# A mixture-of-experts stage between two halves of an attention: fc2's operands exchanged, its result turned on VectorE and stored in 128-byte pieces

## The chip, the cores and the metric

The kernel runs on one core of one Trainium2 chip. The metric is the device time of one execution in microseconds. The kernel before takes 930.86 us, the median of 3 runs (929.11 to 931.17).

## The reference

The input is x, 8 sequences of 1024 tokens with 128 features. It is normalised per token (xn), and the result is the sum of x, of an attention and of a mixture of experts, both of xn:

```
xn  = layernorm(x)
att = gamma * attention(xn) + xn        # 8 heads, q and k of 2 features per head, v of 16,
                                        # scores through leaky relu (0.2), softmax over 1024 keys
# experts: 16 of them, each token goes to its best 2, 1024 slots per expert
xr  = rmsnorm(xn) * norm_weight
probs = softmax(xr @ router.T + router_bias);  gate, expert = top_k(probs, 2)
dispatch[expert, slot] = xr             # 4 experts are trivial (zero, copy, two constant vectors)
h   = gelu(dispatch[4:] @ fc1.T + fc1_bias)          # 12 experts: 1024x128 by 128x512
o   = h @ fc2.T + fc2_bias                           # 1024x512 by 512x128
ffn = sum of the token's two rows of o, weighted by gate / sum of gates
out = x + att + ffn
```

All of it is float32.

## The kernel before

It has five instruction streams written out by hand, one for each engine: the sync engine (`sp`) issues nearly all DMAs in order, GpSimd (`pool`) does the indirect DMAs and the sums into y, ScalarE (`act`) the exponentials and gelus, TensorE (`pe`) the matmuls, and VectorE (`dve`) the rest. Nothing schedules them: on each engine instructions run in the order in which they are written, and the engines wait for each other by semaphores, most of which count instructions or, for a DMA, 16 each.

The program has four stages. A prologue normalises, projects and routes. Then comes the attention of the first three sequences (BH = 3), in which GpSimd scatters the tokens' rows to `disp` in DRAM, 1024 rows of 128 floats per expert. The third stage is the 12 experts. The fourth is the attention of the other five sequences, in which GpSimd gathers the experts' rows from `eout` in DRAM and adds them.

The expert stage is what the change touches. For expert e with u = e % 2:

- The sync engine stores expert e - 2's result and then loads expert e into the buffers of parity u (`store_expert`, `load_expert`, L352 to L367): fc1's weights and fc2's weights, 256 KB each, fc1's bias, fc2's bias spread over all 128 partitions (64 KB), and the expert's rows in four DMAs, each for 32 of the features in pieces of 32 floats (128 bytes). The semaphore `ed0` or `ed1` counts all eight.
- VectorE (`turn_rows`, L1126 to L1133) waits for all of these, multiplies fc1's weights by the norm's weight (L1130) and turns the rows in 32x32 blocks (L1133), so that `xt` holds features in partitions and slots in columns.
- TensorE (`expert`, L880 to L902) multiplies fc1: 8 matmuls with a 128x128 block of weights standing and 512 slots passing (L890); ScalarE takes each through gelu into `hs`, hidden features in partitions and slots in columns (L745). Then fc2: 32 matmuls in which a block of 128 slots of `hs` stands and 128 columns of fc2's weights pass (L901), four to each block of slots, so that the result has slots in partitions.
- VectorE (`expert_rows`, L1138 to L1145) waits for fc2 and for the previous store, and adds the bias from PSUM into `yo` (L1142). This releases the next store.

On VectorE the order in the loop (L1149 to L1152) is: scale and turn expert e + 1, then add expert e's bias. On TensorE the next fc1 follows fc2. In the trace fp32 matmuls stand as two records each.

At the stage's start expert 0 is loaded while the attention still runs. Expert 1 is loaded after the DMAs of `spread` (L328 to L335), 16 small ones that move a pass of attention results between partitions, and after the last value matmul (`pv`). At the end, TensorE computes three score tiles of the next attention between the halves of the last fc2, and VectorE rectifies them (L1112) ahead of the last bias add. `hs`, `yo` and the second row buffer lie in the same memory as the attention's exponentials (`pr`).

Of the kernel before, what the change touches and what calls it, by code (L numbers as in the profile page):

```python
# [8 lines left out]
ALU = mybir.AluOpType  # L9
# [3 lines left out]
P = 128  # L13
B, M, C = 8, 1024, 128
# [10 lines left out]
HALF = 512  # L25
# [9 lines left out]
E, E_MLP, FFN = 16, 12, 512  # L35
FC = FFN // P
CAP = T * 2 // E
SLOTS = E_MLP * CAP
ST = CAP // P
# [22 lines left out]
BLOCK = 32  # L62
NR = P // BLOCK
# [35 lines left out]
    return c  # L99


def build(nc, x, consts, w_qk, b_qk, w_vr, b_v, r_b, n_w, n_w_row, w1t, b1, w2t, b2, cvec, gamma, out):
# [4 lines left out]
    with ExitStack() as ctx:  # L107
        def sb(name, shape, dt=F32):
            return ctx.enter_context(nc.sbuf_tensor(name, shape, dt))

        def sem(name):
# [15 lines left out]
        nwr = sb("nwr", [P, C])  # L127
        gam = sb("gam", [P, 1])
        cv = sb("cv", [P, 2, C])
        b1s = sb("b1s", [P, 2, FC])  # L130
        onesb = sb("onesb", [P, P], BF16)

        bst = sb("bst", [P, NT, 6])
# [47 lines left out]
        gate, rank, at, keep, tmp = (small[:, k:k + 2, :] for k in (4, 6, 8, 10, 12))  # L181


        hs, yo = ef[:, 0:4, :], ef[:, 7, :]
        xt = sb("xt", [P, CAP])
        dd = [xs[:].rearrange("p u t c -> p (u t c)"), ef[:, 5, :]]
        b2s = pflat[:, 0:2 * C].rearrange("p (u c) -> p u c", c=C)
        g1 = xs[:].rearrange("p u (t k) c -> p u t k c", k=2)


# [15 lines left out]
                 "ed0 ed1 w1_rdy xt_rdy fc1 gel fc2 yo_rdy yo_out gath0 gath1 comb final").split()  # L206
        S = {n: sem(n) for n in names}

        block = ctx.enter_context(nc.Block())
# [24 lines left out]
            return slice(2 * HP * (b % 2), 2 * HP * (b % 2) + 2 * HP)  # L234

        ONE = 1
        FROM_ONE = ("gel", "yo_rdy", "yo_out")
        CO0 = 2

        def unit_of(i):  # L240
# [19 lines left out]
        def _(sp):  # L260
# [88 lines left out]
                    spread(p - 1)  # L349
            sp.wait_ge(S["scat"], 16 * GS)  # L350

            def load_expert(e, u):  # L352
                for dst, src in ((w1[:, (2 * u) * FFN:(2 * u + 1) * FFN], w1t[bass.ds(e, 1), :, :].rearrange("a p f -> p (a f)")),
                                 (w1[:, (2 * u + 1) * FFN:(2 * u + 2) * FFN], w2t[bass.ds(e, 1), :, :].rearrange("a p f -> p (a f)")),
                                 (b1s[:, u, :], b1[bass.ds(e, 1), :, :].rearrange("a p f -> p (a f)")),
                                 (b2s[:, u, :], b2[bass.ds(e, 1), :].partition_broadcast(P))):
                    sp.dma_start(dst, src).then_inc(S[f"ed{u}"], 16)
                for q in range(NR):

                    cols = slice(BLOCK * q, BLOCK * q + BLOCK)  # L360
                    sp.dma_start(dd[u][cols, :].rearrange("r (m c) -> r m c", c=BLOCK),
                                 disp[bass.ds(e * CAP, CAP), cols].rearrange("(m r) c -> r m c", r=BLOCK)
                                 ).then_inc(S[f"ed{u}"], 16)

            def store_expert(e):
                sp.wait_ge(S["yo_rdy"], ONE + e + 1)
                sp.dma_start(eout[bass.ds(e * CAP, CAP), :].rearrange("(j p) c -> p j c", p=P),  # L367
                             yo.rearrange("p (j c) -> p j c", c=C)).then_inc(S["yo_out"], 16)

            load_expert(0, 0)  # L370
            spread(BH * NPB - 2)

            sp.wait_ge(S["pv"], BH * NPB * TB)
            load_expert(1, 1)
            with sp.Fori(0, E_MLP // 2 - 1) as k:
                for u in range(2):
                    store_expert(2 * k + u)

                    load_expert(2 * k + u + 2, u)
            for u in range(2):  # L380
                store_expert(E_MLP - 2 + u)

# [13 lines left out]
        def _(pool):  # L396
# [243 lines left out]
            pool.wait_ge(S["yo_out"], ONE + 16 * E_MLP)  # L640
            attention(BH, B, gather)


# [1 line left out]
        def _(act):  # L645
# [81 lines left out]
            def attention(b0, b1):  # L727
                first, end = b0 * NUB, b1 * NUB
                for i in range(first, end):
                    if i == (BUFS - 1) * PAIRS + 1:  # L730
                        act.wait_ge(S["route"], 1)
                    if i == BH * NUB:
                        act.wait_ge(S["fc2"], E_MLP)
                    if i == BH * NUB + (BUFS - 1) * PAIRS:
                        act.wait_ge(S["yo_out"], ONE + 16 * E_MLP)
                    exponentials(i)

            attention(0, BH)
# [24 lines left out]
        def _(pe):  # L763
# [71 lines left out]
            def values(c, half):  # L835

                p, kc = divmod(c, TB)
                hg = p // NQ % NHG
                cols = slice(half * HALF // 2, (half + 1) * HALF // 2)
                pe.wait_ge(S["exps"], PAIRS * (c + 1))  # L840
                if kc == 0 and half == 0:
                    if p == 0:
                        pe.wait_ge(S["at_rdy"], 1)
                    if p == BH * NPB:
                        pe.wait_ge(S["yo_rdy"], ONE + E_MLP)
# [35 lines left out]
            def expert(e, u, first=False, last=False):  # L881
                pe.wait_ge(S["w1_rdy"], e + 1)
                pe.wait_ge(S["xt_rdy"], e + 1)
                for n in range(2 * FC):
                    half, f = n // FC, n % FC

                    pe.wait_ge(S["gel"], ONE + 2 * FC * e + max(n - 3, 0))
                    if n == 2 and first:
                        turn(BH * NPB - 1)
                    pe.matmul(ps[:, 2 + n % 4, :], w1[:, 2 * u * FFN + f * P:2 * u * FFN + (f + 1) * P],  # L890
                              xt[:, half * HALF:(half + 1) * HALF], start=True, stop=True).then_inc(S["fc1"], 1)
                pe.wait_ge(S["turned"], NPB * BH)
                pe.wait_ge(S["yo_rdy"], ONE + e)
                for half in range(2):
                    pe.wait_ge(S["gel"], ONE + 2 * FC * e + FC * (half + 1))
                    if half == 1 and last:
                        ahead(BH, RING)
                    for j in range(half * ST // 2, (half + 1) * ST // 2):
                        o = ps[:, 6 + j // 4, (j % 4) * P:(j % 4 + 1) * P]
                        for f in range(FC):  # L900
                            mm = pe.matmul(o, hs[:, f, j * P:(j + 1) * P],  # L901
                                           w1[:, (2 * u + 1) * FFN + f * P:(2 * u + 1) * FFN + (f + 1) * P],  # L902
                                           start=(f == 0), stop=(f == FC - 1))
                mm.then_inc(S["fc2"], 1)

            ahead(0, AHEAD)
            attention(0, BH)
# [13 lines left out]
        def _(dve):  # L921
# [203 lines left out]

            def turn_rows(e, u):  # L1126

                dve.wait_ge(S[f"ed{u}"], 64 * (e - u) + 128)
# [6 lines left out]
            attention(0, BH)  # L1135


            def expert_rows(e, u):  # L1138

                dve.wait_ge(S["fc2"], e + 1)  # L1140
                dve.wait_ge(S["yo_out"], ONE + 16 * e)
                dve.tensor_tensor(yo.rearrange("p (j c) -> p j c", c=C),  # L1142
                                  ps[:, 6:8, :].rearrange("p a (j c) -> p (a j) c", c=C),
                                  b2s[:, u, :].unsqueeze(1).broadcast_to([P, ST, C]), ALU.add
                                  ).then_inc(S["yo_rdy"], 1)  # L1145

            dve.wait_ge(S["sum_rdy"], 1)
            dve.reciprocal(gsum[:], gsum[:]).then_inc(S["inv_rdy"], 1)
# [12 lines left out]
_INS = ("x", "consts", "w_qk", "b_qk", "w_vr", "b_v", "r_b", "n_w", "n_w_row", "w1t", "b1", "w2t", "b2", "cvec",  # L1161
        "gamma")


def layouts(i):
# [7 lines left out]
    for n, width in (("W", C), ("b", 1)):  # L1173
# [15 lines left out]
        "b1": a["ffn_fc1_bias"].reshape(E_MLP, FC, P).transpose(0, 2, 1),  # L1189
        "w2t": a["ffn_fc2_weight"].transpose(0, 2, 1).reshape(E_MLP, FC, P, C).transpose(0, 2, 1, 3).reshape(E_MLP, P, FC * C),  # L1190
        "b2": a["ffn_fc2_bias"],
        "cvec": a["ffn_constant_vectors"].reshape(1, 2, C),
        "gamma": a["attn_gamma"].reshape(1, 1),
    }
# [18 lines left out]
```

## Time and profile before

| | us |
|---|---|
| median of 3 runs | 930.86 |
| the profiled execution | 931.08 |
| its span, first to last instruction | 929.3 |
| TensorE busy | 851.2 (92%) |
| VectorE busy | 763.9 (82%) |
| ScalarE busy | 676.9 (73%) |
| GpSimd busy | 602.1 (65%) |

The expert stage lies between about 362 and 533 us of the span. A share of busy time over the whole span mixes stages: VectorE is busy almost throughout the attention, and in the expert stage only about a fifth of the time. So the stage is read by itself: by the chain of waits (what each engine was released by), by the engines' instructions in order of time with the idle time ahead of them, and by busy time in short stretches. In these, PEclk is TensorE's granted clock (1.00 is 2.4 GHz), and the DMA share is that of the core's 16 DMA engines.

### The profile page before, as it was taken

The numbers are of one execution on the slowest core, as the hardware profiler recorded it, in microseconds if no ns is written. First come the engines' busy times: TensorE is split into PE (matmuls) and PEld (weight loads), VectorE is DVE, ScalarE is ACT, GpSimd is POOL, SyncE is SP. The second block draws the span as 40 slices with busy tenths as digits, with TensorE's granted clock in tenths as the row PEclk, the third lists the DMA queues.
The fourth block names the chain that finished last, engine by engine and source line by source line (L and its number), as shares of the span: only waits on it lengthen the run. The fifth ranks groups of instructions, "written<-read, shape, count | busy, mean of one in ns | idle before, by whom it ended". The sixth has DMA issues, their size and how long they took to land.

```text
span 929.3 us, 19960 instructions
## 1 busy us (share of the span) xinstructions
PE 851.2 (92%) x7403; PEld 338.5 (36%) x7404; DVE 763.9 (82%) x883; ACT 676.9 (73%) x787; POOL 602.1 (65%) x610
## 2 busy tenths in 40 slices
PE   0687269999999999999999999999999999999997
PEld 0454112222222224776776722222222222222222
DVE  5798899999999996322321399999999999999996
ACT  0578888888888888344344388888888888888886
POOL 3355247777777662999999426567566675766772
PEclk9999669999999999999999999999999999999999
DMA  8733101111111014355364111012112011200202
GB/s 220 301 68 77 31 28 33 49 40 52 50 25 37 21 30 92 88 137 126 86 141 125 40 48 40 21 28 59 29 30 60 25 35 27 77 23 17 68 16 54
DMA packets 130167, 59.34 MB, mean 64 GB/s; under 512 B 83498, under 2 KB 120194, under 8 KB 130080
## 3 DMA queue, kind: packets, MB, share of 16 engines
q1 hardware_dynamic: 120464, 48.06, 20.3%
q0 software_dynamic: 8192, 9.37, 3.7%
q8 instruction: 54, 0.88, 0.4%
q10 hardware_dynamic: 1424, 0.76, 0.4%
q14 instruction: 33, 0.27, 0.1%
HBM read 31.58 MB, written 30.02 MB: 66 GB/s over the span
## 4 chain that ended last, share of the span: by engine, by line
PE 59%; DVE 25%; issue 8%; ACT 3%; POOL 2%; DMA 1%; SPq 1%; POOLq 0%; DVEq 0%; ACTq 0%
DVE ps L1112 20%; PE ps L850 18%; PE ps L830 11%; PE ps L820 11%; PE ps L901 9%; PE ps L890 9%; DVE ot L1088 2%; PE ps L780 1%; DMA y<-in_x 1%; ACT pr L675 1%; DVE bst L947 1%; ACT pr L724 1%; SPq L262 1%; POOL ot L410 1%; ACT va L684 1%
## 5 line engine op out<-in xcount | busy, mean ns | idle before, releaser
L1112 DVE TENSOR_SCALAR ps<-ps 128x1024 f32<-128x1024 f32 x512 | 600.3, 1224 | 15.1 <-PE ps L820 12.1
L724 ACT ACTIVATE pr<-ps 128x1024 f32<-128x1024 f32 x512 | 524.0, 1024 | 104.6 <-PE ps L830 70.7
L850 PE MATMUL ps<-pr,vp 128*32 128x256 f32 x4096 | 327.7, 392 | 0.3
L830 PE MATMUL ps<-q,kz 64*128 64x512 bf16 x1024 | 200.6, 389 | 10.1 <-DVE ps L1112 4.3
L820 PE MATMUL ps<-q,kz 62*128 62x512 bf16 x1024 | 200.8, 390 | 2.9 <-DMA q<-parts_dram 1.4
L511 POOL DMA_INDIRECT xs<-eout,idxs x128 | 129.1, 1008 | 107.5 <-ACT pr L724 82.3
L496 POOL DMA_INDIRECT disp<-xn,idx x128 | 125.8, 983 | 50.4 <-issue 28.2
L745 ACT ACTIVATE pr<-ps,b1s 128x512 f32<-128x512 f32 x96 | 66.0, 687 | 96.4 <-PE ps L890 96.4
L830 PEld LDWEIGHTS ps<-q,kz 64*128 64x128 bf16 x1024 | 48.9, 92 | 226.1 <-DVE ps L1112 187.7
L850 PEld LDWEIGHTS ps<-pr,vp 128*32 128x32 f32 x4096 | 81.1, 108 | 120.5 <-issue 118.1
L1130 DVE TENSOR_SCALAR w<-w,nw 128x512 f32<-128x512 f32 x12 | 14.1, 1175 | 94.6 <-DMA pr<-disp 50.6
L901 PEld LDWEIGHTS ps<-w,pr 128*128 128x128 f32 x768 | 87.7, 192 | 6.2 <-issue 6.2
L820 PEld LDWEIGHTS ps<-q,kz 62*128 62x128 bf16 x1024 | 49.4, 93 | 106.9 <-ACT pr L724 76.7
L901 PE MATMUL ps<-w,pr 128*128 128x128 f32 x768 | 88.0, 275 | 0.0
L890 PE MATMUL ps<-xt,w 128*128 128x512 f32 x192 | 84.7, 593 | 0.6 <-issue 0.6
L634 POOL TENSOR_TENSOR y<-y,xn x24 | 56.6, 2358 | 4.9 <-POOL xn L631 4.9
L531 POOL TENSOR_TENSOR y<-y,xs 128x256 f32<-128x256 f32 x64 | 46.5, 727 | 11.4 <-POOL y L531 5.7
L458 POOL TENSOR_TENSOR y<-y,moved 128x256 f32<-128x256 f32 x32 | 23.3, 730 | 44.3 <-DMA moved<-att 28.5
L890 PEld LDWEIGHTS ps<-xt,w 128*128 128x128 f32 x192 | 35.5, 190 | 40.9 <-issue 40.9
L410 POOL TENSOR_TENSOR ot<-pr,parts 112x512 f32<-112x512 f32 x16 | 18.9, 1179 | 37.3 <-ACT parts L680 37.2
L524 POOL TENSOR_TENSOR xs<-xs,co 128x256 f32<-128x256 f32 x64 | 37.9, 616 | 0.6
L792 PE MATMUL ps<-cst,xn 128*128 128x128 f32 x64 | 10.5, 291 | 27.5 <-DVE xn L966 27.5
(120 smaller groups left out, 527.4 us busy)
## 6 DMA issues: line engine op xcount, KB each, us to landing
moved<-att SPq DMA_DIRECT2D x480, 8.0 KB
disp<-pr SPq DMA_DIRECT2D x12, 512.0 KB, 4.8
eout<-pr SPq DMA_DIRECT2D x12, 512.0 KB, 3.0
y<-in_x SPq DMA_DIRECT2D x8, 512.0 KB, 7.5
out<-y SPq DMA_DIRECT2D x7, 512.0 KB, 3.4
w<-in_w1t SPq DMA_DIRECT2D x12, 256.0 KB, 3.1
w<-in_w2t SPq DMA_DIRECT2D x12, 256.0 KB, 3.3
xs<-disp SPq DMA_DIRECT2D x24, 128.0 KB, 3.5
```

The lines of the kernel that those rows point to most:

```text
L496: pool.indirect_dma_start(out=disp, out_offset=bass.IndirectOffsetOnAxis(ap=idx[:, k, s * TB + t:s * TB + t + 1], axis=0), in_=xn[:, s * T ...
L511: pool.indirect_dma_start(out=g1[:, g % 2, t, c, :], out_offset=None, in_=eout, in_offset=bass.IndirectOffsetOnAxis(ap=idxs[:, c, GB * i + ...
L531: pool.tensor_tensor(yt, yt, rows[:, :, c, :], ALU.add).then_inc(S["comb" if c else "weighted"], 1)
L634: pool.tensor_tensor(yb, yb, xb, ALU.add).then_inc(S["pool_step"], 1)
L724: act.activation(pr[:, c % BUFS, 2 * pair:2 * pair + 2, :], ring[i % RING], ACT.Exp, scale=SLOPE).then_inc(S["exps"], 1)
L745: act.activation(hs[:, f, half * HALF:(half + 1) * HALF], ps[:, 2 + n % 4, :], ACT.Gelu, bias=b1s[:, u, f:f + 1]).then_inc(S["gel"], 1)
L820: last = pe.matmul(ring[i % RING][:, k, :], kz[r:r + ONES, hg, pair, kc * P:(kc + 1) * P], q2[r:r + ONES, hg, qh * HALF:(qh + 1) * HALF], ...
L830: last = pe.matmul(ring[i % RING][:, k, :], kz[r:r + TILE, hg, pair, kc * P:(kc + 1) * P], q2[r:r + TILE, hg, qh * HALF:(qh + 1) * HALF], ...
L850: last = pe.matmul(acc[p % 2][32 * g:32 * g + 32, cols], vp[:, hg, kc, g, :], pr[:, c % BUFS, g % PAIRS * 2 + g // PAIRS, cols], start=(kc ...
L890: pe.matmul(ps[:, 2 + n % 4, :], w1[:, 2 * u * FFN + f * P:2 * u * FFN + (f + 1) * P], xt[:, half * HALF:(half + 1) * HALF], start=True, s ...
L901: mm = pe.matmul(o, hs[:, f, j * P:(j + 1) * P], w1[:, (2 * u + 1) * FFN + f * P:(2 * u + 1) * FFN + (f + 1) * P], start=(f == 0), stop=(f ...
L1112: dve.tensor_scalar(s, s, 0.0, 1.0 / SLOPE - 1.0, ALU.max, ALU.mult).then_inc(S["relu"], 1)
```

## The change

fc2 exchanges its operands: a 128x128 block of fc2's weights stands, and 512 slots of `hs` pass. Its result then has output features in partitions and slots in columns, one PSUM bank for each half of the slots. VectorE adds the bias, now one value per partition, half by half into a new buffer `ob` (in the memory of `pr`), and turns each half in 32x32 blocks into `yo`. A full transpose needs more than turned blocks: block (i, j) still stands at place (i, j), so the store puts it right, in four DMAs of 32 partitions each, in pieces of 32 floats (128 bytes). fc2's bias joins fc1's as a fifth column (`b12`), so its own broadcast load goes away and seven loads make an expert. A new semaphore `biased` counts halves, frees the PSUM banks for TensorE, and lies between a half's bias add and its turn. Expert 1's weights and biases are loaded ahead of the 16 DMAs of `spread`; its rows stay behind them.

```
-            load_expert(0, 0)
+            load_weights(0, 0)
+            load_rows(0, 0)
+            load_weights(1, 1)
             spread(BH * NPB - 2)
             sp.wait_ge(S["pv"], BH * NPB * TB)
-            load_expert(1, 1)
+            load_rows(1, 1)
             with sp.Fori(0, E_MLP // 2 - 1) as k:
                 for u in range(2):
                     store_expert(2 * k + u)
-                    load_expert(2 * k + u + 2, u)
+                    load_weights(2 * k + u + 2, u)
+                    load_rows(2 * k + u + 2, u)
...
             def store_expert(e):
-                sp.wait_ge(S["yo_rdy"], ONE + e + 1)
-                sp.dma_start(eout[bass.ds(e * CAP, CAP), :].rearrange("(j p) c -> p j c", p=P),
-                             yo.rearrange("p (j c) -> p j c", c=C)).then_inc(S["yo_out"], 16)
+                sp.wait_ge(S["yo_rdy"], e + 1)
+                for q in range(NR):
+                    cols = slice(BLOCK * q, BLOCK * q + BLOCK)
+                    sp.dma_start(eout[bass.ds(e * CAP, CAP), cols].rearrange("(m r) c -> r m c", r=BLOCK),
+                                 yo[cols, :].rearrange("r (m c) -> r m c", c=BLOCK)).then_inc(S["yo_out"], 16)
...
-                pe.wait_ge(S["yo_rdy"], ONE + e)
+                pe.wait_ge(S["biased"], ONE + 2 * e)
                 for half in range(2):
                     pe.wait_ge(S["gel"], ONE + 2 * FC * e + FC * (half + 1))
                     if half == 1 and last:
                         ahead(BH, RING)
-                    for j in range(half * ST // 2, (half + 1) * ST // 2):
-                        o = ps[:, 6 + j // 4, (j % 4) * P:(j % 4 + 1) * P]
-                        for f in range(FC):
-                            mm = pe.matmul(o, hs[:, f, j * P:(j + 1) * P],
-                                           w1[:, (2 * u + 1) * FFN + f * P:(2 * u + 1) * FFN + (f + 1) * P],
-                                           start=(f == 0), stop=(f == FC - 1))
-                mm.then_inc(S["fc2"], 1)
+                    for f in range(FC):
+                        mm = pe.matmul(ps[:, 6 + half, :],
+                                       w1[:, (2 * u + 1) * FFN + f * P:(2 * u + 1) * FFN + (f + 1) * P],
+                                       hs[:, f, half * HALF:(half + 1) * HALF], start=(f == 0), stop=(f == FC - 1))
+                    mm.then_inc(S["fc2"], 1)
...
+            def expert_half(e, u, half):
+                cols = slice(half * HALF, (half + 1) * HALF)
+                dve.wait_ge(S["fc2"], 2 * e + half + 1)
+                dve.tensor_scalar(ob[:, cols], ps[:, 6 + half, :], b1s[:, u, FC:FC + 1], None, ALU.add
+                                  ).then_inc(S["biased"], 1)
+                if half == 0:
+                    dve.wait_ge(S["yo_out"], ONE + 16 * NR * e)
+                dve.wait_ge(S["biased"], ONE + 2 * e + half + 1)
+                ins = dve.transpose(yo[:, cols], ob[:, cols])
+                if half == 1:
+                    ins.then_inc(S["yo_rdy"], 1)
+
             def expert_rows(e, u):
-                dve.wait_ge(S["fc2"], e + 1)
-                dve.wait_ge(S["yo_out"], ONE + 16 * e)
-                dve.tensor_tensor(yo.rearrange("p (j c) -> p j c", c=C),
-                                  ps[:, 6:8, :].rearrange("p a (j c) -> p (a j) c", c=C),
-                                  b2s[:, u, :].unsqueeze(1).broadcast_to([P, ST, C]), ALU.add
-                                  ).then_inc(S["yo_rdy"], 1)
+                for half in range(2):
+                    expert_half(e, u, half)
...
             turn_rows(E_MLP - 1, 1)
             expert_rows(E_MLP - 2, 0)
+            expert_half(E_MLP - 1, 1, 0)
             for i in range(BH * NUB, BH * NUB + RING):
                 rectify(i)
-            expert_rows(E_MLP - 1, 1)
+            expert_half(E_MLP - 1, 1, 1)
```

The first place is the sync engine's loop, one pass of which serves two experts; here from a store to the last load of rows behind it, in the kernel before. The rows named ISA set an address register.

```order
L367 DMA eout<-pr 128x8x128
L357 ISA
L357 DMA w<-in_w1t 128x512
L357 DMA w<-in_w2t 128x512
L357 ISA
L357 DMA b1s<-in_b 128x4
L357 ISA
L357 DMA parts<-in_b 128x128
L361 ISA
L361 DMA xs<-disp 32x32x32
```

And the same place in the changed kernel (`eout<-pr` is again the store, `b1s<-in_b` now carries both biases):

```order
L370 DMA eout<-pr 32x32x32
L370 ISA
L370 DMA eout<-pr 32x32x32
L370 ISA
L370 DMA eout<-pr 32x32x32
L370 ISA
L370 DMA eout<-pr 32x32x32
L355 ISA
L355 DMA w<-in_w1t 128x512
L355 DMA w<-in_w2t 128x512
L355 ISA
L355 DMA b1s<-in_b 128x5
```

Three more issues stand ahead of the weights, and one fewer (`parts<-in_b`) between the weights and the rows.

The second place is VectorE's loop, the first of its two experts, in the kernel before: scale and turn of the next expert, then the bias add of this one.

```order
L1130 TENSOR_SCALAR w<-w,nw 128x512
L1132 ISA
L1133 STREAM_TRANSPOSE xt<-pr 128x1024
L1141 ISA
L1142 TENSOR_TENSOR pr<-ps,parts 128x1024
```

And in the changed kernel, where `pr<-ps,b1s` is a half's bias add into `ob` and `pr<-pr` its turn into `yo`:

```order
L1133 TENSOR_SCALAR w<-w,nw 128x512
L1135 ISA
L1136 STREAM_TRANSPOSE xt<-pr 128x1024
L1144 ISA
L1145 TENSOR_SCALAR pr<-ps,b1s 128x512
L1148 ISA
L1149 REGISTER_ALU
L1150 STREAM_TRANSPOSE pr<-pr 128x512
L1145 TENSOR_SCALAR pr<-ps,b1s 128x512
L1149 REGISTER_ALU
L1150 STREAM_TRANSPOSE pr<-pr 128x512
```

Both halves stand behind the next expert's scale and turn; the one add has become four instructions.

The third is the sync engine at the stage's start, in the kernel before, where `moved<-att` is `spread`:

```order
L357 DMA w<-in_w1t 128x512
L357 DMA w<-in_w2t 128x512
L357 DMA b1s<-in_b 128x4
L357 DMA parts<-in_b 128x128
L361 DMA xs<-disp 32x32x32 x4
L334 DMA moved<-att 32x64 x16
L357 DMA w<-in_w1t 128x512
L357 DMA w<-in_w2t 128x512
L357 DMA b1s<-in_b 128x4
L357 DMA parts<-in_b 128x128
L361 DMA pr<-disp 32x32x32 x4
```

And in the changed kernel:

```order
L355 DMA w<-in_w1t 128x512
L355 DMA w<-in_w2t 128x512
L355 DMA b1s<-in_b 128x5
L361 DMA xs<-disp 32x32x32 x4
L355 DMA w<-in_w1t 128x512
L355 DMA w<-in_w2t 128x512
L355 DMA b1s<-in_b 128x5
L333 DMA moved<-att 32x64 x16
L361 DMA pr<-disp 32x32x32 x4
```

Expert 1's three loads of weights and biases now stand ahead of the 16 small DMAs, and its rows alone behind them.

## Rows read from the trace of the kernel before

**Rows 1.** The chain of waits, expert stage: start us, length us, what.

```profile
377.22 0.59 issue
...
384.91 7.14 PE ps L901 x64
392.06 6.87 PE ps L890 x16
...
518.18 6.87 PE ps L890 x16
...
529.37 3.78 PE ps L901 x32
533.15 0.40 issue
```

**Rows 2.** Busy time by stretch, one expert: us, engines, PEclk, DMA share, GB/s.

```profile
391.89:405.90 14.01, 14.01 (x82) 10.18 (x81) 3.25 (x3) 5.50 (x8) 12.68 (x7) 1.00 0.50 117
```

**Rows 3.** VectorE's groups by line, 380 to 517 us: busy, mean ns, idle before.

```profile
L1130 DVE TENSOR_SCALAR w<-w,nw 128x512 f32<-128x512 f32 x10 | 11.2, 1121 | 86.6 <-DMA xs<-disp 44.0 <-DMA pr<-disp 42.6
L1142 DVE TENSOR_TENSOR pr<-ps,parts 128x1024 f32<-128x1024 f32 x9 | 11.0, 1225 | 17.1 <-PE ps L901 17.1
L1133 DVE STREAM_TRANSPOSE xt<-pr 128x1024 f32<-128x1024 f32 x5 | 6.2, 1230 | 0.0
```

**Rows 4.** VectorE's groups by line and shape, whole trace.

```profile
L1088 DVE STREAM_TRANSPOSE ot<-ps 128x512 f32<-128x512 f32 x30 | 21.2, 706 | 0.0
L984 DVE TENSOR_REDUCE kmax<-ps 128x1 f32<-128x512 f32 x16 | 10.9, 684 | 0.3 <-PE ps L801 0.2
```

**Rows 5.** VectorE in order of time: start us, us, line, [idle before <-releaser].

```profile
374.15 2.41 DVE L1130 TENSOR_SCALAR w<-w,nw 128x512 f32<-128x512 f32 x1 [8.01 <-DMA pr<-disp]
...
377.64 1.18 DVE L1142 TENSOR_TENSOR pr<-ps,parts 128x1024 f32<-128x1024 f32 x1
...
430.33 0.99 DVE L1130 TENSOR_SCALAR w<-w,nw 128x512 f32<-128x512 f32 x1 [8.88 <-DMA pr<-disp]
...
485.83 0.54 DVE L1130 TENSOR_SCALAR w<-w,nw 128x512 f32<-128x512 f32 x1 [8.34 <-DMA pr<-disp]
...
504.30 1.23 DVE L1142 TENSOR_TENSOR pr<-ps,parts 128x1024 f32<-128x1024 f32 x1 [2.33 <-PE ps L901]
513.98 1.08 DVE L1130 TENSOR_SCALAR w<-w,nw 128x512 f32<-128x512 f32 x1 [8.46 <-DMA pr<-disp]
514.98 1.23 DVE L1133 STREAM_TRANSPOSE xt<-pr 128x1024 f32<-128x1024 f32 x1
```

**Rows 6.** The sync engine's DMA issues in order of time.

```profile
355.21 10.02 SPq L334 DMA_DIRECT2D moved<-att  x16
...
367.32 4.87 SPq L361 DMA_DIRECT2D pr<-disp  x4
...
421.64 0.42 SPq L367 DMA_DIRECT2D eout<-pr  x1
...
505.72 0.42 SPq L367 DMA_DIRECT2D eout<-pr  x1
...
508.13 0.33 SPq L357 DMA_DIRECT2D parts<-in_b  x1
508.66 3.15 SPq L361 DMA_DIRECT2D pr<-disp  x4
```

**Rows 7.** Busy time by stretch, with DMA share and GB/s in the last columns.

```profile
351.40:355.30 3.90, 3.90 (x44) 1.10 (x44) 3.90 (x5) 3.30 (x4) 0.00 (x0) 1.00 0.78 131
...
520.50:522.00 1.50, 1.50 (x5) 0.69 (x4) 0.00 (x0) 1.16 (x3) 1.50 (x1) 1.00 1.12 338
```

**Rows 8.** GpSimd and ScalarE in order of time, around the stage's two ends.

```profile
366.57 1.41 POOL L458 TENSOR_TENSOR y<-y,moved 128x256 f32<-128x256 f32 x2 [15.46 <-DMA moved<-att]
...
519.67 2.35 POOL L637 TENSOR_TENSOR y<-y,bvg 128x1024 f32 x1 [0.19 <-POOL y L634]
...
540.52 2.18 ACT L724 ACTIVATE pr<-ps 128x1024 f32<-128x1024 f32 x2 [0.74 <-PE ps L830]
```

More of the change, by code:

```diff
@@ L99, in constants, with build @@
     return c
-def build(nc, x, consts, w_qk, b_qk, w_vr, b_v, r_b, n_w, n_w_row, w1t, b1, w2t, b2, cvec, gamma, out):
+def build(nc, x, consts, w_qk, b_qk, w_vr, b_v, r_b, n_w, n_w_row, w1t, b12, w2t, cvec, gamma, out):
     parts_dram = nc.dram_tensor("parts_dram", [2, NROW * H, T], BF16, kind="Internal").ap()
@@ L129, in build @@
         cv = sb("cv", [P, 2, C])
-        b1s = sb("b1s", [P, 2, FC])
+        b1s = sb("b1s", [P, 2, FC + 1])
         onesb = sb("onesb", [P, P], BF16)
@@ L181, in build @@
         gate, rank, at, keep, tmp = (small[:, k:k + 2, :] for k in (4, 6, 8, 10, 12))
-        hs, yo = ef[:, 0:4, :], ef[:, 7, :]
+        hs, ob, yo = ef[:, 0:4, :], ef[:, 4, :], ef[:, 7, :]
         xt = sb("xt", [P, CAP])
         dd = [xs[:].rearrange("p u t c -> p (u t c)"), ef[:, 5, :]]
-        b2s = pflat[:, 0:2 * C].rearrange("p (u c) -> p u c", c=C)
         g1 = xs[:].rearrange("p u (t k) c -> p u t k c", k=2)
@@ L205, in build @@
                  "scat staged pool_step carry "
-                 "ed0 ed1 w1_rdy xt_rdy fc1 gel fc2 yo_rdy yo_out gath0 gath1 comb final").split()
+                 "ed0 ed1 w1_rdy xt_rdy fc1 gel fc2 biased yo_rdy yo_out gath0 gath1 comb final").split()
         S = {n: sem(n) for n in names}
@@ L236, in build @@
         ONE = 1
-        FROM_ONE = ("gel", "yo_rdy", "yo_out")
+        FROM_ONE = ("gel", "biased", "yo_out")
         CO0 = 2
@@ L350, in _, with load_weights, load_rows @@
             sp.wait_ge(S["scat"], 16 * GS)
-            def load_expert(e, u):
+            def load_weights(e, u):
                 for dst, src in ((w1[:, (2 * u) * FFN:(2 * u + 1) * FFN], w1t[bass.ds(e, 1), :, :].rearrange("a p f -> p (a f)")),
                                  (w1[:, (2 * u + 1) * FFN:(2 * u + 2) * FFN], w2t[bass.ds(e, 1), :, :].rearrange("a p f -> p (a f)")),
-                                 (b1s[:, u, :], b1[bass.ds(e, 1), :, :].rearrange("a p f -> p (a f)")),
-                                 (b2s[:, u, :], b2[bass.ds(e, 1), :].partition_broadcast(P))):
+                                 (b1s[:, u, :], b12[bass.ds(e, 1), :, :].rearrange("a p f -> p (a f)"))):
                     sp.dma_start(dst, src).then_inc(S[f"ed{u}"], 16)
+            def load_rows(e, u):
                 for q in range(NR):
@@ L638, in _ @@
                                    ).then_inc(S["pool_step"], 1)
-            pool.wait_ge(S["yo_out"], ONE + 16 * E_MLP)
+            pool.wait_ge(S["yo_out"], ONE + 16 * NR * E_MLP)
             attention(BH, B, gather)
@@ L732, in attention @@
                     if i == BH * NUB:
-                        act.wait_ge(S["fc2"], E_MLP)
+                        act.wait_ge(S["fc2"], 2 * E_MLP)
                     if i == BH * NUB + (BUFS - 1) * PAIRS:
-                        act.wait_ge(S["yo_out"], ONE + 16 * E_MLP)
+                        act.wait_ge(S["yo_out"], ONE + 16 * NR * E_MLP)
                     exponentials(i)
@@ L844, in values @@
                     if p == BH * NPB:
-                        pe.wait_ge(S["yo_rdy"], ONE + E_MLP)
+                        pe.wait_ge(S["biased"], ONE + 2 * E_MLP)
                     pe.wait_ge(S["vp_rdy"], p // NQ + 1)
@@ L1126, in turn_rows @@
             def turn_rows(e, u):
-                dve.wait_ge(S[f"ed{u}"], 64 * (e - u) + 128)
+                dve.wait_ge(S[f"ed{u}"], 56 * (e - u) + 112)
                 rows = w1[:, 2 * u * FFN:(2 * u + 1) * FFN]
@@ L1154, in _ @@
             expert_rows(E_MLP - 2, 0)
+            expert_half(E_MLP - 1, 1, 0)
             for i in range(BH * NUB, BH * NUB + RING):
                 rectify(i)
-            expert_rows(E_MLP - 1, 1)
+            expert_half(E_MLP - 1, 1, 1)
             attention(BH, B, RING)
-_INS = ("x", "consts", "w_qk", "b_qk", "w_vr", "b_v", "r_b", "n_w", "n_w_row", "w1t", "b1", "w2t", "b2", "cvec",
+_INS = ("x", "consts", "w_qk", "b_qk", "w_vr", "b_v", "r_b", "n_w", "n_w_row", "w1t", "b12", "w2t", "cvec",
         "gamma")
@@ L1188, in layouts @@
         "w1t": a["ffn_fc1_weight"].transpose(0, 2, 1),
-        "b1": a["ffn_fc1_bias"].reshape(E_MLP, FC, P).transpose(0, 2, 1),
+        "b12": np.concatenate([a["ffn_fc1_bias"].reshape(E_MLP, FC, P).transpose(0, 2, 1), a["ffn_fc2_bias"].reshape(E_MLP, C, 1)], axis=2),
         "w2t": a["ffn_fc2_weight"].transpose(0, 2, 1).reshape(E_MLP, FC, P, C).transpose(0, 2, 1, 3).reshape(E_MLP, P, FC * C),
-        "b2": a["ffn_fc2_bias"],
         "cvec": a["ffn_constant_vectors"].reshape(1, 2, C),
```

## The prediction

> **What bounds the kernel now.** I read the chain of waits first. Through the expert stage, from 362 to 533 us, it names TensorE alone: per expert 6.87 us of fc1 (L890) and 7.14 us of fc2 (L901), 14.01 together, and only once a gap, 0.59 us before expert 1 [rows 1]. The stage runs at a granted clock of 1.00, so at 2.4 GHz [rows 2]. The reader is to see how little lies behind that. Ahead of every fc1 VectorE must have scaled fc1's weights (L1130) and turned the rows (L1133), both wait for that expert's eight loads, and the loads stand on the sync queue behind the store of the expert two before, which waits for VectorE's bias add (L1142). This is a ring through VectorE and the sync queue, one turn per expert, and I price it from the timeline:
>
> - Store issued to the landing of the loads behind it: 421.64 to 430.33 is 8.69 us, 505.72 to 513.98 is 8.26; over the seven such stores in between and at the ends the mean is 8.44 [rows 5, 6].
> - Scaling and turning: 1.12 + 1.23 us, which overlap by 0.08 (513.98 + 1.08 against 514.98): 2.27 [rows 3, 5].
> - Bias add 1.23, and 0.19 from its end (504.30 + 1.23) to the store's issue [rows 5, 6].
>
> That is 12.13 us, 1.88 less than the 14.01 that TensorE needs. VectorE's own idle time says the same from the other side: ahead of nine bias adds it waited 17.1 us for fc2, 1.90 each [rows 3]. So 1.9 us per expert is all that a longer ring may cost before TensorE starts to wait.
>
> **The change, part by part.**
>
> *fc2 in 512-column matmuls.* Per expert 32 matmuls of 128 columns (64 records) become 8 of 512, the shape and number of fc1's. So fc2 should take fc1's 6.87 us: 0.27 less per expert, 3.2 over twelve, if TensorE stays the bound. Its period would then be 13.74.
>
> *Bias and turn on VectorE.* One add of 1.23 us is replaced by four instructions of 512 columns: two bias adds out of PSUM, two transposes. The nearest rows are a 128x512 transpose at 0.706 and a 128x512 pass over PSUM at 0.684 [rows 4], so 1.39 per half, 1.42 with the wait of the turn for its own bias add; 2.84 for both. Bounds: 1.23 per half (half of two 1024-column instructions, no gap) and 1.5. The first half could run under the second half of fc2, but on VectorE it is queued behind the scaling and turning of the next expert, as the order of VectorE's instructions shows. As soon as the loads of that expert land late, nothing of the 2.84 is hidden. The ring grows by 1.61, and 0.27 of its spare time is left against 14.01; against 13.74 nothing is. The wait for the previous store to land, which moves from the add to the first turn, costs nothing: that store was issued a whole turn of the ring earlier.
>
> *The store.* One issue of 512 KB becomes four of 128 KB in pieces of 128 bytes, and one load, the 64 KB bias broadcast, goes away. All of it stands on the sync queue ahead of the next-but-one expert's loads, which thus wait for it twice, for its issue and for its transfer. As to issues: three more and one less, at one slot of 0.53 us (508.13 to 508.66), is +1.1 at least; but the four loads in 128-byte pieces took 3.15 us to issue, so if the stores do likewise it is 3.15 - 0.53 - 0.53 = +2.1 [rows 6]. As to transfer: the 512-byte store moves in 1.50 us at 338 GB/s, the same amount loaded in 128-byte pieces in 3.90 us at 131 GB/s; the trace has no store in such pieces. At the loads' rate it is +2.4, less 0.2 for the 64 KB at 338 GB/s, +2.2 [rows 7]. I take +2.0, next to the two that agree. Bounds: 0, as if pieces cost nothing, and 6.1, twice the loads' transfer.
>
> The Trainium skill bears on that bound: "DMA: Bandwidth & Descriptors", Specifications, says that below 512 B the DMA engine does a read-modify-write. By that page the store would read and write each piece, which is the upper bound; that small pieces are slow the trace shows for loads, a read-modify-write no row here shows. The same page, "Why small descriptors are slow", gives a fixed overhead of about 3 cycles a packet beside one for 32 bytes. By it four pieces would take 28 cycles where one 512-byte packet takes 19, an estimate of 2.2 us for the store and of +0.5 for the ring; the loads' 3.90 us speak against so small a price.
>
> *Second expert's weights early.* They move ahead of 16 small DMAs whose issue takes 10.02 us [rows 6]. Expert 1's rows are issued after the same set of issues as before, without two bias broadcasts of 0.53 us, so at about 366.3 instead of 367.32. They take 5.3 (508.66 to 513.98) to 6.8 us (367.32 to 374.15) to land; 6.1 gives 372.4 [rows 5, 6]. Scaling, here 2.41, and turning end at 376.0, before fc2 of expert 0 ends (377.22 - 0.27 = 376.95). So the 0.59 gap goes, and expert 1 starts 0.86 earlier, at 376.95 and not 377.81 [rows 1]. The 16 moved DMAs are issued some 1.5 us later; GpSimd, which had idled 15.46 us for them, starts its stage work later by as much and ends it near 523.5 instead of 522.0, long before the stage's end [rows 8].
>
> *The sum.* VectorE is free at 376.0 and both halves of expert 0 end at 378.8, as the add did (377.64 + 1.18). The store goes out at 379.0, expert 2's loads land at 379.0 + 8.44 + 2.0 = 389.4, its rows are turned at 391.7, fc1 starts at 391.8; it did at 392.06. From there the ring sets the pace: 10.44 + 2.27 + 2.84 + 0.19 = 15.74 us per expert, 2.0 more than TensorE's 13.74. Nine turns to expert 11 are 141.7 us. For the last two GpSimd is done, and I take 0.54 for the scaling, the value of one that ran fast at 485.83 [rows 5], which takes off 1.2: 140.5. Before, it was 518.18 - 392.06 = 126.1 [rows 1]. So +14.4; less 0.25 at the start of expert 2, less 0.27 for the last fc2, plus 0.2 because a half with its turn (1.42) and not the add of 1.23 stands ahead of the fourth rectification: +14.1. Against the profiled execution's 931.08 that is 945.2; the median lies 0.2 below it, so 945.0.
>
> The end of the stage costs no more. The last store lands some 1.4 + 0.2 + 5.3 = 6.9 us after fc2 ends. ScalarE needs it for its seventh exponential, which ran at 541.6, 8.4 us after fc2's end at 533.15 [rows 1, 8]. Per 1 us on the store, ten loads are later, so about 10 us on the total.
>
> **The rivals.**
>
> *TensorE stays the bound (13%), faster.* If the pieces cost the store almost nothing, so that at most 0.3 us is added, and a half is 1.23, then the ring is 13.5 to 13.8 and TensorE's 13.74 decides. The gain is 3.2 + 0.6 us: 927. For it speaks that stores may be acknowledged otherwise than loads; against it the 1.1 us of issues, which only do not count while the queue has data left to move.
>
> *A small price (12%).* The store adds 0.3 to 1.1 us, as its transfer begins with its first quarter. Then the ring is 14.0 to 14.8: 929 to 936, with no change in the middle of it.
>
> *Writes in pieces are dearer than reads (13%).* At 7.8 us of transfer the store adds 6.1, the ring is 19.8, and the total is 945 + 41 = 986; halfway, at 4.0, 965. It decides from the point where a piece written costs more than one read. For it: stores were in 512 bytes or more so far, so nothing shows the contrary. Against it: the loads have the same pieces on the same queue.
>
> *Ring as priced (62%).* With the store's +1.1 to +2.7 (issue and transfer in part added): 936 to 952.
>
> **How the numbers follow.** A measurement of this kernel can tell 0.2%, 929.0 to 932.7, from no change. Faster: the first rival and a little of the second, 14%. Same: 6%. Slower: 80%. The range from 929 to 962 leaves out the first rival and the upper half of the third, some 20%; the likeliest case's own range is 936 to 952.
>
> **What would show it.** fc2's eight matmuls at about 6.87 us per expert; four VectorE instructions of 0.7 us; ahead of each fc1 from expert 3 on TensorE idle by 1.5 to 2.5 us, released by the transpose of the rows; VectorE waiting, ahead of the scaling, for the loads, and not for fc2 ahead of the bias adds. From the first store issue to the landing some 10.4 us. I am wrong if fc1 follows fc2 without a gap, which would say that the store costs under 0.3 us, or if the gap is there and the landing unchanged, which would say that it is VectorE's queue alone.

## The result, and the profile after

The changed kernel takes 953.86 us, the median of 6 runs (952.28 to 955.53), against 931.01 for the kernel before in the same comparison: a ratio of 1.0244, with a 95% interval of 1.0227 to 1.0262. That is 22.9 us slower; 14 were forecast. It lies inside the stated range of 929 to 962, but above the 936 to 952 of the case held likeliest. The profiled execution took 953.69 us.

TensorE, which had no gap after expert 1 [rows 1], now waits ahead of fc1. These are its waits in the expert stage (who waited for whom: us in total, times, longest):

```profile
PE ps L895 <- DVE xt L1136: 15.7, 8, 2.8
PE ps L895 <- issue: 3.2, 2, 1.7
```

And VectorE's, from 380 to 545 us:

```profile
DVE w L1133 <- DMA xs<-disp: 57.5, 5, 12.1
DVE w L1133 <- DMA pr<-disp: 57.0, 5, 11.6
```

VectorE no longer waits for fc2 ahead of its bias adds, as it did for 17.1 us [rows 3]. It waits for the loads alone: the ring of store, loads, scale and turn, bias adds sets the pace. One turn of it in the order of VectorE's instructions (start us, us, what, idle before):

```profile
490.64 1.48 DVE L1133 TENSOR_SCALAR w<-w,nw 128x512 f32<-128x512 f32 x1 [11.43 <-DMA xs<-disp]
492.04 1.23 DVE L1136 STREAM_TRANSPOSE xt<-xs 128x1024 f32<-128x1024 f32 x1
493.20 0.70 DVE L1145 TENSOR_SCALAR pr<-ps,b1s 128x512 f32<-128x512 f32 x1
493.94 0.71 DVE L1150 STREAM_TRANSPOSE pr<-pr 128x512 f32<-128x512 f32 x1
494.58 0.71 DVE L1145 TENSOR_SCALAR pr<-ps,b1s 128x512 f32<-128x512 f32 x1
495.32 0.71 DVE L1150 STREAM_TRANSPOSE pr<-pr 128x512 f32<-128x512 f32 x1
```

The second bias add follows the first turn at once; fc2 had ended long before. The sync queue's side of that turn, up to the next store:

```profile
479.39 2.61 SPq L370 DMA_DIRECT2D eout<-pr  x4
482.20 0.81 SPq L355 DMA_DIRECT2D w<-in_w1t  x1
...
484.48 3.02 SPq L361 DMA_DIRECT2D xs<-disp  x4
...
496.21 2.69 SPq L370 DMA_DIRECT2D eout<-pr  x4
```

The loads behind the first store issue at 479.39 have landed at 490.64, 11.25 us later; in the turn of [rows 5, 6] it had been 8.26, and the means over ten turns are 11.27 and 8.47. The four stores took 2.61 us to issue where the one had taken 0.42, and the rows are issued 5.09 us after the first store issue instead of 2.94. What the queue moves in the time: first the rows of this turn, then a store with nothing behind it, that of expert 10, issued from 543.80 on (busy time by stretch; the last columns are PEclk, DMA share and GB/s):

```profile
486.00:489.50 3.50, 3.50 (x9) 1.52 (x8) 0.00 (x0) 0.00 (x0) 2.99 (x3) 1.00 1.18 152
544.70:548.50 3.80, 3.80 (x11) 1.65 (x10) 0.00 (x0) 3.07 (x5) 0.00 (x0) 1.00 0.88 136
```

The store in 128-byte pieces needs 3.8 us at 136 GB/s, hardly more than the rows' loads in such pieces, 3.5 at 152; the 512-byte store had taken 1.5 at 338 [rows 7].

The forecast prices of the instructions came out. Groups of VectorE, 380 to 535 us (busy, mean ns, idle before), and then those of TensorE over the whole trace, the last line being fc2 in the kernel before:

```profile
L1150 DVE STREAM_TRANSPOSE pr<-pr 128x512 f32<-128x512 f32 x18 | 12.8, 712 | 0.6
L1145 DVE TENSOR_SCALAR pr<-ps,b1s 128x512 f32<-128x512 f32 x18 | 12.7, 706 | 0.0
L1133 DVE TENSOR_SCALAR w<-w,nw 128x512 f32<-128x512 f32 x9 | 10.4, 1155 | 103.4 <-DMA xs<-disp 57.5 <-DMA pr<-disp 45.9
```

```profile
L895 PE MATMUL ps<-xt,w 128*128 128x512 f32 x192 | 90.4, 625 | 18.9 <-DVE xt L1136 15.7
L904 PE MATMUL ps<-pr,w 128*128 128x512 f32 x192 | 84.6, 593 | 0.0
```

```profile
L901 PE MATMUL ps<-w,pr 128*128 128x128 f32 x768 | 88.0, 275 | 0.0
```

A bias add takes 0.706 and a turn 0.712 us, 2.83 for a whole expert with the gaps, against 2.84 forecast. fc2 (L904) is busy for 84.6 us instead of 88.0: it did become as fast as fc1, and nothing comes of it.

### The profile page after: what moved, and what is told of

It is laid out like the page before. It is cut to its first block and busy times, and to the rows that moved or that the text cites. A ratio compares the mean times of both kernels' runs of the same rounds, so it can differ in the third digit from the quotient of the medians.

```text
span 951.9 us, 18941 instructions
## 1 busy us (share of the span) xinstructions
PE 854.1 (90%) x6827; PEld 289.5 (30%) x6828; DVE 779.1 (82%) x919; ACT 676.9 (71%) x787; POOL 602.1 (63%) x610
## 5 line engine op out<-in xcount | busy, mean ns | idle before, releaser
L1133 DVE TENSOR_SCALAR w<-w,nw 128x512 f32<-128x512 f32 x12 | 11.8, 987 | 120.5 <-DMA pr<-disp 63.0
L895 PE MATMUL ps<-xt,w 128*128 128x512 f32 x192 | 90.4, 625 | 18.9 <-DVE xt L1136 15.7
L904 PE MATMUL ps<-pr,w 128*128 128x512 f32 x192 | 84.6, 593 | 0.0
L904 PEld LDWEIGHTS ps<-pr,w 128*128 128x128 f32 x192 | 36.4, 190 | 45.9 <-issue 45.9
```

Source lines behind the costliest of these rows:

```text
L904: mm = pe.matmul(ps[:, 6 + half, :], w1[:, (2 * u + 1) * FFN + f * P:(2 * u + 1) * FFN + (f + 1) * P], hs[:, f, half * HALF:(half + 1) * H ...
```

## The experiments

The theory is the ring. Its length per expert is the sum of these parts: from the first store issue to the landing of the loads, plus scaling, plus 1.15 (the turn of the rows without its overlap), plus the bias adds and turns, plus 0.19 to the next issue. TensorE's 14.01 us (13.74 with the new fc2) decides where the ring is shorter. The rivals are VectorE's four instructions by themselves, fc2's shape or TensorE's clock, and the early weights. In the table, landing and scaling are means over the ten stores that have loads behind them, and the period is measured from the first of the ten scalings to the last:

| run | landing | scaling | ring by the sum | period | median us | ratio to before (95%) |
|---|---|---|---|---|---|---|
| before | 8.47 | 1.12 | 12.2 | 14.06 | 931.01 | |
| changed | 11.27 | 1.09 | 16.5 | 16.53 | 953.86 | 1.0227 to 1.0262 |
| store_one | 9.09 | 1.14 | 14.4 | 14.34 | 932.41 | 1.0010 to 1.0033 |
| one_bias_first | 9.26 | 0.86 | 14.3 | 14.18 | 933.60 | 1.0013 to 1.0045 |
| store_four_512 | 9.88 | 0.88 | 14.9 | 14.88 | 941.84 | 1.0098 to 1.0135 |
| store_four_256 | 10.51 | 1.72 | 16.4 | 16.48 | 953.32 | 1.0215 to 1.0277 |
| before_store_128 | 10.60 | 1.24 | 14.4 | 14.83 | 939.40 | 1.0056 to 1.0102 |
| half_first | 11.15 | 0.69 | 14.6 | 14.58 | 941.03 | 1.0087 to 1.0151 |
| late_weights | 11.14 | 1.13 | 16.4 | 16.42 | 953.22 | 1.0218 to 1.0275 |
| rows_early | 7.54 | 1.16 | 12.9 | 13.71 | 927.86 | 0.9952 to 0.9981 |
| before_rows_early | | | | | 930.10 | 0.9978 to 1.0007 |
| rows_early_half | | | | | 933.44 | 1.0021 to 1.0048 |

Landing, scaling and period belong to the one profiled execution; the median of all executions can differ from it by a few us where the ring decides. In rows_early, where the rows no longer stand behind the store, the landing is that of the biases. For the last two runs only the time is given.

**store_one: the store as one DMA in 512-byte pieces.**

```
-                for q in range(NR):
-                    cols = slice(BLOCK * q, BLOCK * q + BLOCK)
-                    sp.dma_start(eout[bass.ds(e * CAP, CAP), cols].rearrange("(m r) c -> r m c", r=BLOCK),
-                                 yo[cols, :].rearrange("r (m c) -> r m c", c=BLOCK)).then_inc(S["yo_out"], 16)
+                sp.dma_start(eout[bass.ds(e * CAP, CAP), :].rearrange("(j p) c -> p j c", p=P),
+                             yo.rearrange("p (j c) -> p j c", c=C)).then_inc(S["yo_out"], 16)
... (and the counts of the three waits for yo_out)
```

> The changed kernel with the result stored by one DMA in 512-byte pieces, as the kernel before does it; the rows then land in the wrong places of the expert's block, and nothing else differs. Theory (the store in 128-byte pieces lengthens the ring through VectorE and the sync queue): from store to the landing of the loads 11.27 us falls to about 8.2, the ring to 8.2 + 2.3 + 2.8 + 0.2 = 13.5 us, under TensorE's 13.74, so TensorE sets the pace again and the total is about 928 (926 to 932). Rival (the four instructions on VectorE are what costs): the landing falls but the time stays at 950 or above. Rival (fc2 in its new shape or TensorE's clock costs): fc2 or fc1 stay longer than 6.9 us and the time stays above 940.

It took 932.41 us: 21 of the 23 us go with the store's form. The chain of waits (start us, us, what) still runs round the ring in the middle of the stage and reaches TensorE alone at its end:

```profile
395.71 1.09 SPq L355
...
399.87 3.76 DMA pr<-disp
404.49 1.23 DVE xt L1133
...
513.10 6.87 PE ps L901 x16
```

fc2's 6.87 us is there, but the landing fell to 9.09 only and not to 8.2, so the ring is 14.4 and not 13.5, and the total lies just above what was expected (926 to 932). With the store as it was before, the loads still land 0.62 us later than the 8.47 of the kernel before: that much of the longer landing does not come from the store.

**store_four_512 and store_four_256: four issues, larger pieces.**

```
-                    cols = slice(BLOCK * q, BLOCK * q + BLOCK)
-                    sp.dma_start(eout[bass.ds(e * CAP, CAP), cols].rearrange("(m r) c -> r m c", r=BLOCK),
-                                 yo[cols, :].rearrange("r (m c) -> r m c", c=BLOCK)).then_inc(S["yo_out"], 16)
+                    rows = slice(BLOCK * q, BLOCK * q + BLOCK)
+                    sp.dma_start(eout[bass.ds(e * CAP + q * CAP // NR, CAP // NR), :].rearrange("(m r) c -> r m c", r=BLOCK),
+                                 yo[rows, :].rearrange("r (m c) -> r m c", c=C)).then_inc(S["yo_out"], 16)
```

(the other has half as wide columns, `c=C // 2`, in two column halves)

> The changed kernel with four store DMAs as it has, each of 32 partitions, but in pieces of 512 bytes; the rows land in the wrong places. It tells the number of issues from the size of the pieces. If the pieces cost: transfer 1.5 us instead of 4.2, only the three more issues remain, at most 3 x 0.53 = 1.6 and less where the queue still moves data; ring 13.7 to 15.0, total 929 to 943, 933 taken. If the issues cost as much as the pieces: ring 16.4, total 950 or more.

> The changed kernel with its four store DMAs in pieces of 256 bytes, half as many as in 128; the values land in the wrong places. With 512-byte pieces (1024 of them) the loads behind the store landed 9.88 us after its first issue, with 128-byte pieces (4096) 11.27. If the cost goes with the number of pieces: 10.35 (2048 pieces), ring 15.5, total about 946 (944 to 949). If it is a threshold under 512 bytes: 11.3 and 953. If pieces of 256 bytes still move at full rate: 9.9 and 942.

store_four_512 took 941.84, near the top of its 929 to 943 and far from the 933 taken; store_four_256 took 953.32 where 944 to 949 was expected, a miss. Landing by landing the price is clear: four DMAs of 32 partitions in place of one of 128 +0.79 (9.09 to 9.88), pieces of 256 bytes +0.63 more, of 128 bytes +0.76 more. No run tells the three more issues from the fewer partitions of each. By the total alone, 256 bytes would have passed for a threshold: 953.32 is as slow as the changed kernel. That is a coincidence, and the groups of the scaling show it, first of the run with 256 bytes and then of the one with 512:

```profile
L1134 DVE TENSOR_SCALAR w<-w,nw 128x512 f32<-128x512 f32 x10 | 17.2, 1722 | 106.9 <-DMA pr<-disp 53.5 <-DMA xs<-disp 53.4
```

```profile
L1133 DVE TENSOR_SCALAR w<-w,nw 128x512 f32<-128x512 f32 x10 | 8.8, 876 | 100.6 <-DMA xs<-disp 50.4 <-DMA pr<-disp 50.2
```

The scaling took 1.72 us instead of 0.88, though it is the same instruction on the same data. GpSimd and VectorE at one such scaling in the 256-byte run:

```profile
474.37 1.90 POOL L637 TENSOR_TENSOR xn<-cv,co 128x1024 f32 x1 [0.26 <-POOL y L640]
```

```profile
474.75 1.79 DVE L1134 TENSOR_SCALAR w<-w,nw 128x512 f32<-128x512 f32 x1 [10.77 <-DMA pr<-disp]
```

GpSimd's instruction ends at 476.27, the scaling at 476.54. In the 512-byte run, GpSimd's ended just after the scaling became ready:

```profile
480.04 1.90 POOL L636 TENSOR_TENSOR xn<-cv,co 128x1024 f32 x1 [0.26 <-POOL y L639]
```

```profile
481.81 0.49 DVE L1133 TENSOR_SCALAR w<-w,nw 128x512 f32<-128x512 f32 x1 [9.80 <-DMA xs<-disp]
```

The traces of all runs show the same: a scaling takes 0.49 us by itself, and one that starts while GpSimd is in an instruction ends 0.27 to 0.30 us after that instruction, unless its own 0.49 end later. One that began 0.04 us ahead of a GpSimd instruction waited it out too (2.66 us, store_four_512). VectorE's bias adds from PSUM and its turns kept their 0.71 beside the same work. So the scaling's share of the ring depends on where the ring's period lands in GpSimd's, and my expectation, which held the scaling fixed, missed.

**before_store_128: the kernel before with the store alone in 128-byte pieces.**

```
-                sp.dma_start(eout[bass.ds(e * CAP, CAP), :].rearrange("(j p) c -> p j c", p=P),
-                             yo.rearrange("p (j c) -> p j c", c=C)).then_inc(S["yo_out"], 16)
+                for q in range(NR):
+                    cols = slice(BLOCK * q, BLOCK * q + BLOCK)
+                    sp.dma_start(eout[bass.ds(e * CAP, CAP), cols].rearrange("(j p) c -> p j c", p=P),
+                                 yo.rearrange("p (j c) -> p j c", c=C)[:, :, cols]).then_inc(S["yo_out"], 16)
... (and the counts of the three waits for yo_out)
```

> The kernel before, with its store alone cut into four DMAs in 128-byte pieces to the same places. Theory: the ring of 12.13 us grows by 2.8 to 3.0 to about 15.1, past TensorE's 14.01, ten times: total about 942 (939 to 945). Rival (VectorE's four instructions cost, not the store): the ring keeps under 14.01 and the total stays at 931. Rival (small pieces cost only together with the new shape): 931 too.

It took 939.40, near the 942 expected: the store alone, without the new fc2 and without VectorE's extra work, makes TensorE wait.

```profile
PE ps L893 <- DVE xt L1136: 4.7, 3, 2.2
```

The landing grew by 2.13 us, from 8.47 to 10.60, and not by the 2.8 to 3.0 expected; so the ring is 14.4, and it exceeds TensorE's 14.01 in some turns only. The period of 14.83 is longer than both: 4.7 us of waits, and some 1.7 us for an fc1 that took 8.82 in place of 7.1 after one of them, come on top of TensorE's own time (TensorE in order of time; the last section returns to this):

```profile
424.13 8.82 PE L893 MATMUL ps<-xt,w 128*128 128x512 f32 x16 [2.20 <-DVE xt L1136]
```

**half_first: VectorE's first half ahead of the next expert's scale and turn.**

```
-                    turn_rows(2 * k + u + 1, 1 - u)
-                    expert_rows(2 * k + u, u)
+                    expert_half(2 * k + u, u, 0)
+                    turn_rows(2 * k + u + 1, 1 - u)
+                    expert_half(2 * k + u, u, 1)
... (and the same order for the last two experts)
```

> The changed kernel with VectorE's order in the loop changed: first half's bias add and turn of this expert, then the next expert's scale and turn, then the second half. If the VectorE part of the ring counts as priced, 1.42 us of 16.4 leave it, ten times: about 940 (938 to 943). If only the store counts and the halves are hidden: 953, no change.

941.03 (937.02 to 945.08 in four executions), as expected: 12.8 us for 1.42 us taken out of each turn and, in the profiled execution, which is the fastest of the four, scalings that met GpSimd less (0.69). So VectorE's part does count, with the store as it is.

```profile
433.20 0.75 DVE L1145 TENSOR_SCALAR pr<-ps,b1s 128x512 f32<-128x512 f32 x1 [9.46 <-PE ps L904]
...
435.14 0.49 DVE L1133 TENSOR_SCALAR w<-w,nw 128x512 f32<-128x512 f32 x1 [0.44 <-DMA pr<-disp]
...
436.70 0.71 DVE L1145 TENSOR_SCALAR pr<-ps,b1s 128x512 f32<-128x512 f32 x1
```

**late_weights: expert 1's weights behind the 16 small DMAs again.**

> The changed kernel without the early load of expert 1's weights: they stand behind the 16 small DMAs again, ahead of its rows. Theory: expert 1's rows land 1 to 2 us later, VectorE's halves of expert 0 and so the first store 0.6 to 1.5 us later, and the ring carries that to the end: about 955 (954.3 to 955.5). Rival (the first store waits for fc2, not for expert 1's rows): no change, 953.9.

953.22, no change: the rival was right. In both orders the first store waits for fc2 of expert 0; VectorE's second half waited for it for 1.83 us in the changed kernel and 1.2 us here:

```profile
DVE pr L1145 <- PE ps L904: 1.2, 1, 1.2
```

**rows_early and before_rows_early: the rows loaded as soon as their buffer is free.**

```
                 for u in range(2):
+                    sp.wait_ge(S["xt_rdy"], 2 * k + u + 1)
+                    load_rows(2 * k + u + 2, u)
                     store_expert(2 * k + u)
                     load_weights(2 * k + u + 2, u)
-                    load_rows(2 * k + u + 2, u)
```

> The changed kernel with the four loads of an expert's rows issued as soon as their buffer is free (the turn of the expert two before), ahead of the store instead of behind the weights; the store stays in 128-byte pieces. Theory: the ring then ends with the landing of the weights, about 7 us after the store's first issue instead of 11.27, so it is 7 + 2.3 + 2.8 + 0.2 = 12.3 us, under TensorE's 13.74; TensorE sets the pace and fc2's new shape shows its gain: about 927.5 (926 to 930). Rival (the moved transfers collide with the store and weights, the DMA queue being the limit): 940 or more.

> The kernel before with the same move of the row loads and nothing else. Theory: TensorE sets its pace already, so the shorter ring gains nothing: 930.5, within 0.2%. Rival (the move is worth something by itself, whatever fc2's shape): 2 us or more faster.

Both came out: 927.86, which beats the kernel before (0.9967, interval 0.9952 to 0.9981) with the store still in 128-byte pieces, and 930.10 against 930.3 (0.9992, interval 0.9978 to 1.0007) for the move by itself. With early rows VectorE's waits are for the small bias load, the last behind the store, and for fc2 again, and TensorE has no idle time ahead of fc1 or fc2 (last column):

```profile
DVE w L1134 <- DMA b1s<-in_b: 77.2, 10, 8.2
DVE pr L1146 <- PE ps L905: 18.4, 10, 8.8
```

```profile
L896 PE MATMUL ps<-xt,w 128*128 128x512 f32 x192 | 84.6, 593 | 0.0
L905 PE MATMUL ps<-pr,w 128*128 128x512 f32 x192 | 84.6, 593 | 0.0
```

**rows_early_half: both changes together.** The edit of half_first on top of rows_early.

> The row loads moved as in the run with early rows, and VectorE's first half ahead of the next expert's scale and turn. Theory: the ring is already under TensorE's period, so taking another 1.4 us off it gains nothing: equal to the run with early rows within 1 us, about 927.5. Rival (the ring still decides in some of the turns): 1 to 4 us faster than that run.

933.44, 5.6 us slower than rows_early: a miss, and the rival did not foresee it either. The chain of waits shows it:

```profile
385.08 3.45 PE ps L905 x8
388.53 0.03 issue
388.55 0.76 DVE pr L1146
...
389.97 1.29 DVE w L1134
391.26 1.17 DVE xt L1137
...
392.66 7.13 PE ps L896 x16
```

The scale and turn of the next expert are now behind a half that cannot start before half of fc2 is done, so fc1 starts 0.7 us after fc2's end (388.53 + 3.45). This scaling met GpSimd and took 1.29 us; at 0.49 the turn would have ended before fc2 did, an estimate from these rows. With a long ring this order pays; with a short one it takes away the lead that the turn had.

**one_bias_first: store_one with the bias load ahead of the weights.**

> The run with one store DMA in 512-byte pieces, with the load of the two biases (128 pieces of 20 bytes) ahead of the weights instead of between weights and rows. In that run the loads still landed 9.0 us after the store and not 8.44 as before the change. If the small load between weights and rows is what holds the rows up: landing 8.5, ring 13.7, total 928 to 930. If not: landing 9.0, 932.4 unchanged.

933.60, landing 9.26: not the cause. What holds the rows in store_one up stays open. In store_one the queue has moved all but the last pieces by 402.5 us, and VectorE starts 1.16 us later (busy time by stretch, then VectorE):

```profile
402.00:402.50 0.50, 0.50 (x3) 0.22 (x2) 0.00 (x0) 0.00 (x0) 0.23 (x2) 1.00 0.95 84
402.50:403.00 0.50, 0.50 (x2) 0.19 (x1) 0.00 (x0) 0.00 (x0) 0.50 (x1) 1.00 0.01 1
```

```profile
403.66 0.91 DVE L1130 TENSOR_SCALAR w<-w,nw 128x512 f32<-128x512 f32 x1 [9.27 <-DMA pr<-disp]
```

In the kernel before, data moves until 513.7 us and the scaling starts at 513.98 [rows 5]:

```profile
513.50:513.75 0.25, 0.25 (x4) 0.25 (x4) 0.00 (x0) 0.00 (x0) 0.25 (x1) 1.00 0.39 73
513.75:514.00 0.25, 0.25 (x5) 0.25 (x4) 0.02 (x1) 0.00 (x0) 0.25 (x1) 1.00 0.00 0
```

Over ten turns the loads land 0.3 us after the last data in the kernel before and in before_store_128, and 0.8 to 1.0 us after it in each of the seven runs of the changed kernel that load the rows last, the changed kernel itself among them. So it belongs to something in the change other than the store, and no run shows to what.

## Why the prediction was right, and where it was short

- *TensorE has 1.9 us to spare and no more*: right. With fc2's new shape its own period is 13.74; with the ring at 14.4 (store_one) it waits a little, at 12.9 (rows_early) not at all.
- *VectorE's four instructions*: 2.83 us against 2.84, and queued behind the next expert's turn, as forecast.
- *The store, +2.0*: right. It measured 2.13 by itself (before_store_128, 10.60 against 8.47) and 2.18 within the change (11.27 against store_one's 9.09). The two estimates, up to 2.1 from issues and 2.2 from transfer, were taken for two views of one delay, and that held: their sum of 4.3 is not what was measured.
- *The landing, 8.44 + 2.0 = 10.44*: the term that was mis-sized, by 0.8. It measured 11.27. The prediction changed the store in it and nothing else; but 0.6 us more stand there with the old store too (9.09 in store_one against 8.47), between the queue's last data and the landing. What makes them is open. Ten landings at 0.83 are 8.3 us. The fc1 of expert 0 also started 0.76 later (363.26 against 362.50), before anything that the change does to the ring, and the first store went out at 379.41 and not at 379.0; 14.1 + 8.3 + 0.4 is 22.8, where the two profiled executions are 22.6 apart (953.69 and 931.08).
- *The range*: held partly by luck. The total lies above the likeliest case's 952, in the part that the range had for writes dearer than reads; that rival did not come true, and the 0.6 us had no rival.
- *fc2's gain of 3.2*: real and hidden, as forecast; rows_early lets it out. There it comes to 2.4 by the medians, and to 2.2 against before_rows_early.
- *A write dearer than a read*: the rule of the Trainium skill that below 512 bytes the DMA engine does a read-modify-write ("DMA: Bandwidth & Descriptors", Specifications) would have made the store about 7.8 us by the prediction's reckoning. It took 3.8 at 136 GB/s, the loads of the same pieces 3.5 to 3.9. So small stores cost about what small loads cost here, not twice; whether a read is part of either no run shows. The step from 256 to 128 bytes costs as much again (0.76 us) as that from 512 to 256 (0.63), which a threshold alone would not do.
- *Early weights, 0.86*: no gain from the order. The old gap of 0.59 ahead of expert 1 is gone in both orders. It came with a scaling of 2.41 us [rows 5], which in the changed kernel took 0.48, with the weights early, and 0.83 with them late.

## What to carry to other kernels

An engine that is busy without a gap says nothing of how near the next ring is: add up the ring's parts, compare with the busy engine's period, and price every edit against the difference. Measure one part of an edit from both sides, alone on the old kernel and taken out of the new one: here both gave 2.1 to 2.2 us for the store, and what the landing grew beyond that has another cause. A load that waits only for a buffer should not stand behind a store that waits for a result.

## What the runs showed of the hardware

- VectorE's scaling, SBUF to SBUF in float32, does not share with GpSimd: it waits out the instruction that GpSimd is in. The Trainium skill ("SBUF — State Buffer", Who interferes with whom) says that the two contend for a shared pair of ports, held for a whole instruction, when VectorE runs in certain modes, which `tensor_scalar` can enter; the 0.49 to 2.66 us of one and the same scaling agree, and the 0.71 of bias adds and turns beside GpSimd show that not all of VectorE's instructions do.
- TensorE's granted clock fell in some of the fc1 that followed a wait, and not in others. After 2.83 us of waiting one took 8.82 us: its clock was 0.50, which is 1.2 GHz, for some 3 us and then 1.00 again, 2.4 GHz. In the same trace one after 2.63 us of waiting took 7.13, and one after 2.21 us took 8.83, so the length of the wait alone does not say which. The ring hid it here; in before_store_128 an fc1 of 8.82 us stood in the chain that set the pace and lengthened the run. TensorE in order of time, then by stretch (the third number from the end is the clock):

```profile
426.95 7.13 PE L895 MATMUL ps<-xt,w 128*128 128x512 f32 x16 [2.63 <-DVE xt L1136]
...
493.51 8.82 PE L895 MATMUL ps<-xt,w 128*128 128x512 f32 x16 [2.83 <-DVE xt L1136]
```

```profile
494.00:497.00 3.00, 3.00 (x5) 1.21 (x4) 2.00 (x3) 0.69 (x1) 2.55 (x3) 0.50 0.00 0
497.50:502.00 4.50, 4.50 (x12) 2.05 (x11) 0.00 (x0) 3.47 (x6) 4.13 (x3) 1.00 0.93 167
```
